# An attention and expert kernel: the first transposed score of a unit goes ahead of the burst of the product with V on TensorE

## The chip, the cores and the metric

The kernel runs on one core of a Trainium2 chip. Its time is the device time of one execution in microseconds (us), the median of three runs. TensorE (PE) does matrix products and transpositions into the eight PSUM banks, VectorE (DVE) reductions and elementwise work, ScalarE (ACT) exponentials and copies, GpSimd (POOL) smaller elementwise work and gathers, and SyncE (SP) issues DMAs. Each engine executes its own program in the written order and waits on semaphores that others raise.

## The reference

```python
def _L0_attn_ref(content, Wq, Wk, Wv):          # content: 4 x 1024 x 256, 16 heads of 16
    Q = (content @ Wq).reshape(b, n, HEADS, HEAD_DIM)
    K = (content @ Wk).reshape(b, n, HEADS, HEAD_DIM)
    V = (content @ Wv).reshape(b, n, HEADS, HEAD_DIM)
    scores = jnp.einsum('bqhd,bkhd->bhqk', Q, K) / math.sqrt(HEAD_DIM)
    alpha = jax.nn.softmax(scores, axis=-1)      # over all keys
    alpha = jnp.where(causal, alpha, 0)          # the mask comes after the softmax
    return jnp.einsum('bhqk,bkhd->bqhd', alpha, V).reshape(b, n, d)
...
x = x + _layernorm(_L0_attn_ref(_layernorm(x), Wq, Wk, Wv))
x = x + _layernorm(_L0_ffn_ref(_layernorm(x), router_w, w_fc, w_proj))
```

`_L0_ffn_ref` is a layer of 8 experts, of which each token uses its best 2 (256 to 1024, exact gelu, back to 256). Since the mask comes after the softmax, maxima and sums run over all 1024 keys, also those above the diagonal.

## The kernel before

**Parts of the program.** A prologue normalizes x and makes Q, K and V in eight chunks; the attention starts within it. The attention runs until about 950 us, with its last groups mixed with the router's work. Then 71 tiles of 128 tokens go through the experts, and the results are added and written.

**Groups and units.** The 64 pairs of batch and head are taken in 16 groups of four heads (`GH`). A pass p of the loop (`groups`, `body`) has 32 units k (`U`). In a unit the engines work on two or three groups at once: plain scores and maxima of group p, transposed scores and the product with V of group p-1 or p-2. `live` says whether a group exists for that. `due(at, k)` gives the numbers of a table that fall into unit k and how many passes back their group is. So the tables `at_chunk`, `at_piece`, `at_m`, `at_poc` and `at_turn` set which unit does what, and the text of `body` on each engine sets the order within a unit.

**What a unit does on PE** (`body` in `block.tensor`):
- at two units of 32 a *turn* (L1313): the finished product with V is transposed;
- at twelve of 32 a *burst* (`pieces`, L1168): one block of 128 keys of four heads times V, in fp32, four heads side by side in 32 columns of the array each, into bank 7. The bursts are numbered 0 to 11 and stand in units 13, 16, 18, 21, 24, 26, 29, and 0, 2, 5, 8, 10 of the next pass. It waits for the exponentials (`s_expB`), for masked copies of POOL (`s_mask`), and at numbers 0 and 8, which start a new half, for DVE's copy of bank 7 (`s_poc`, made at L1760);
- the first *transposed score* (`chunk(p, u, *todo[0])`, L1140), here called A: keys x queries, 512 columns, bf16;
- the pair of *plain scores* of one head and 128 queries (L1326), here S, into banks 0 and 1 or 2 and 3 by turns. It waits for the maximum of two units before (`s_max`). DVE takes the row maximum of the pair (L1786);
- at units 1, 9, 17 and 25 the *transposition of the maxima* of one head (L1337), whose three bf16 parts POOL has made (L762 to L768). ACT copies it out (L962), POOL spreads it (L775) into extra rows of Q, by which a transposed score comes out with its maximum subtracted;
- the second transposed score, here B (L1140, or L1133, a corner of which only the sum is wanted).

ACT takes the exponential of every transposed score: L979 into SBUF for the product, L974 in place for the corners, with the sum by an accumulator read. In its own program of a unit the copy of the maxima (L962) stands ahead of the exponentials of A and B.

**The ring of banks.** A, B, the turns and the transposed maxima share banks 4, 5 and 6. `ring_entries` lists them in the order turn, A, maxima, B for each unit, and `ring_banks` gives each the bank that was used longest ago. Before a matmul into such a bank `ring_free` waits for whoever reads the earlier entry: `s_expB` (exponential), `s_mtc` (copy of the maxima) or `s_norm` (the turn's reader). As a rule the bank is that of the third entry before. A turn keeps its bank for four more entries. The list holds no bursts, which have bank 7.

In a unit without maxima the entries are A, B; so the third entry before an A is the B of two units before. Behind a unit with maxima, whose entries are A, maxima, B, it is the A of that unit. Bursts 2, 5, 8 and 11 are in units 18, 26, 2 and 10, each directly behind one with maxima.

Of the kernel before, what the change touches and what calls it, by code (L numbers as in the profile page):

```python
# [5 lines left out]
def sandwich(nc, x_d, wq_d, wk_d, wv_d, router_d, wfc_d, wproj_d, out_d):  # L6
# [41 lines left out]
    with ctx:  # L48
# [169 lines left out]
        def bk(i):  # L218
            return ps[:, i, :]
# [138 lines left out]
        def diagonal(b):  # L358

            i, hf = BURSTS[b]  # L360
            return hf == i // 4
# [10 lines left out]
        def chunk_of(b, hl):  # L372

            n = GH * b + hl
            return 4 * (n // 3) + n % 3

        def is_corner(c):

            return c % 4 == 3
# [9 lines left out]
        def segments(b, piece):  # L389

            up = upper(b)
            out = [("n", 0, up)] if up else []
            if up < 512:
                out.append(("v", up, 512))
            if diagonal(b):
                out.append(("d", up - P, up))
            return out
# [6 lines left out]
        def due(at, k):  # L404

            return [(n, x // U) for n, x in enumerate(at) if x % U == k]
# [3 lines left out]
        def live(p, back):  # L410

            return not isinstance(p, int) or 0 <= p - back < NGR
# [66 lines left out]
        def wait_pos(eng, s, v):  # L479

            if isinstance(v, int) and v <= 0:
                return
            eng.wait_ge(s, v)
# [58 lines left out]
        def ring_bank(kind, g, x):  # L542

            return RING_BANK[kind, g, x]
# [533 lines left out]
        def _(pe):  # L1078
# [36 lines left out]
            def ring_free(kind, g, x):  # L1115
                if RING_USER[kind, g, x] is None:
                    return
                last, g, x = RING_USER[kind, g, x]
                if last == "chunk":
                    pe.wait_ge(s_expB, NCH * g + x + 1)  # L1120
                elif last == "turn":
                    pe.wait_ge(s_norm, 2 * g + x + 1)
                else:
                    pe.wait_ge(s_mtc, GH * g + x + 1)

            def chunk(p, u, c, back):
                if not live(p, back):
                    return
                g, v = p - back, (u - back) % NSL
                ring_free("chunk", g, c)  # L1130
                if is_corner(c):
                    hl, i = divmod(c // 4, HQ)
                    nc.tensor.matmul(bk(ring_bank("chunk", g, c)), qs[v][0:MROW + MR, hl, i * P:(i + 1) * P],  # L1133
                                     ks[v][0:MROW + MR, hl, 512:1024], start=True, stop=True).then_inc(s_ST, 1)
                    return
                b, hl = divmod(3 * (c // 4) + c % 4, GH)
                i, hf = BURSTS[b]
                if b == 0:
                    pe.wait_ge(s_ex, GH * g + hl + 1)
                nc.tensor.matmul(bk(ring_bank("chunk", g, c)), ks[v][0:MROW + MR, hl, i * P:(i + 1) * P],  # L1140
                                 qs[v][0:MROW + MR, hl, hf * 512:(hf + 1) * 512],
                                 start=True, stop=True).then_inc(s_ST, 1)

            def pieces(p, u, k):
                for n, back in due(at_piece, k):
                    if not live(p, back):
                        continue
                    b, piece = divmod(n, NPC)
                    g, v, (i, hf) = p - back, (u - back) % NSL, BURSTS[b]
                    et, out = et_sb[b % NET], bk(7)  # L1150
                    if isinstance(g, int) and g == 0 and n == 0:
                        pe.wait_ge(s_poz, 1)
                    if b == 0 and piece == 0:
                        pe.wait_ge(s_vc, g + 1)
                    if i == 0 and piece == 0:
                        j = HALVES.index(hf)
                        wait_pos(pe, s_poc, 2 * g + j)
                    if piece == 0:
                        pe.wait_ge(s_expB, NCH * g + (chunk_of(b, GH - 1) + 1))
                    for n, (kind, q0, q1) in enumerate(segments(b, piece)):  # L1160
                        if kind == "d":
                            pe.wait_ge(s_mask, NDG * g + sum(diagonal(x) for x in range(b + 1)))
                        for hl in range(GH):
                            rows, lhs, rhs = {
                                "v": (VW, vh[v][:, hl, i, :], et[:, hl, q0:q1]),
                                "n": (VW, vone[:, :], et[:, hl, q0:q1]),
                                "d": (DH, vh[v][:, hl, i, 0:DH], md_sb[b % NET][:, hl, :])}[kind]
                            ins = nc.tensor.matmul(out[32 * hl:32 * hl + rows, q0:q1], lhs, rhs,  # L1168
                                                   start=(i == 0 and piece == 0 and n == 0), stop=False, skip_group_check=True)
                    if piece == NPC - 1:  # L1170
                        ins.then_inc(s_pv, 1)
# [117 lines left out]
            def body(p, u, units=range(U)):  # L1289
                for k in units:  # L1290
                    if at_tail(AT_LIST, p, k):
                        list_early()
                    for g in tail(at_count, p, k):
                        count(g)
                    if at_tail(AT_TURN0, p, k):
                        transpose_x(0, 0)
                    for hf in range(2):
                        if at_tail(AT_FIRST[hf], p, k):
                            first_half(0, 0, hf)
                    for n in tail(at_turn_x, p, k):  # L1300
                        turn_x(*divmod(n, KC))
                    for i in tail(at_logits, p, k):
                        logits(i)
                    for i in tail(at_back, p, k):
                        turn_back(i)
                    for j, back in due(at_turn, k):
                        if not live(p, back):
                            continue
                        hf = HALVES[j]
                        pe.wait_ge(s_poc, 2 * (p - back) + (j + 1))  # L1310
                        ring_free("turn", p - back, j)
                        for t in range(HQ):
                            ins = nc.tensor.transpose(bk(ring_bank("turn", p - back, j))[:, t * P:(t + 1) * P],  # L1313
                                                      po_sb[:, (HQ * hf + t) * P:(HQ * hf + t + 1) * P], ident[:, :])
                        ins.then_inc(s_T4, 1)
                    pieces(p, u, k)
                    todo = due(at_chunk, k)
                    chunk(p, u, *todo[0])
                    if live(p, 0):
                        hl, i = divmod(k, QT)  # L1320
                        if k == 0:
                            pe.wait_ge(s_ld[u], 16 * 2 * TERMS * ((p - u) // NSL + 1) if isinstance(p, int) else
                                       (16 * 2 * TERMS // NSL) * (p + (NSL - u)))
                        wait_pos(pe, s_max, U * p + k - 1)
                        for hf in range(2):
                            ins = nc.tensor.matmul(bk(2 * (k % 2) + hf), qs[u][0:SROWS, hl, i * P:(i + 1) * P],  # L1326
                                                   ks[u][0:SROWS, hl, hf * 512:(hf + 1) * 512], start=True, stop=True)
                        ins.then_inc(s_S, 1)
                    for hl, back in due(at_m, k):
                        if not live(p, back):  # L1330
                            continue
                        h = GH * (p - back) + hl
                        pe.wait_ge(s_sp, 4 * h + 4)
                        turned[0] += 1
                        if p - back:
                            ring_free("maxima", p - back, hl)
                        nc.tensor.matmul(bk(turn_bank(hl, p - back))[MROW:MROW + MR, 0:P],  # L1337
                                         mparts[:, hl % 2].rearrange("p s i -> p (s i)"), identb[:, :],
                                         start=True, stop=True).then_inc(s_mtp, 1)
                    for c, back in todo[1:]:  # L1340
                        chunk(p, u, c, back)
# [630 lines left out]
```

## Time and profile before

| | |
|---|---|
| median of three runs | 1500.67 us (1499.77 to 1502.28) |
| profiled execution | 1502.44 us, its span 1500.5 us |
| mean granted TensorE clock | 0.979 |
| busy: PE, DVE, ACT, POOL | 93%, 60%, 54%, 42% of the span |
| attention's steady part, 400 to 600 us, busy of 200 us | PE 192.87, DVE 177.80, ACT 162.57, POOL 99.58 |
| one group of heads, 391.76 to 440.04 us | 48.28 us |
| expert part, 1040 to 1100 us | PE busy 60.00 of 60 us |

A row of the timeline gives start, length, engine, line, operation, output <- input, and how many instructions are merged in it. A bracket tells how long the engine had idled before it and what ended that. PE's ends are modelled: a matmul of 512 columns shows 0.38 us, though the next one starts 0.22 us behind it. So on PE distances are read from start to start.

### The profile page before, as it was taken

To read this page: it belongs to the slowest core of one execution; us is meant where nothing else is said; L and a number is where in the kernel's file an instruction comes from. 1 tells how busy PE (TensorE), PEld (TensorE's weight loads), DVE (VectorE), ACT (ScalarE), POOL (GpSimd) and SP (SyncE) were. 2 spreads that over 40 slices of the span, in tenths; PEclk is the share of its full clock that TensorE was granted. 3 is DMA by queue.
4 is the path that set the end of the run, shared out by engine and by line. 5 is a ranking of instruction groups with operands and counts; after the bars stand their busy time and mean duration, and the time that the engine had idled before them with its cause. 6 is when DMAs were issued, how large, how long until landed. Compare 5 with 4: busy or idle time off the path is not lost.

```text
span 1500.5 us, 28701 instructions
## 1 busy us (share of the span) xinstructions
PE 1388.9 (93%) x9774; PEld 828.8 (55%) x9775; DVE 903.0 (60%) x1710; ACT 807.1 (54%) x1757; POOL 625.9 (42%) x749
## 2 busy tenths in 40 slices
PE   6788899999999999999999987999999999999990
PEld 3444233333333333333333333999999999999980
DVE  4587788888988898889988977751111111111115
ACT  4454777777887878888888885311111111111114
POOL 3244444544454545544454523333333333333325
PEclk9999999999999999999999998999999999999995
DMA  3766732023320333122322243666666666666647
GB/s 119 163 156 137 253 43 43 12 33 43 43 35 9 43 43 44 17 27 43 43 35 65 63 136 121 173 171 180 182 189 180 176 179 178 188 188 175 178 113 227
DMA packets 100405, 166.85 MB, mean 111 GB/s; under 512 B 12400, under 2 KB 67568, under 8 KB 100304
## 3 DMA queue, kind: packets, MB, share of 16 engines
q1 hardware_dynamic: 86192, 146.08, 36.6%
q0 software_dynamic: 13632, 18.69, 7.7%
q10 hardware_dynamic: 480, 0.79, 0.3%
q8 instruction: 56, 0.92, 0.3%
q14 instruction: 45, 0.37, 0.1%
HBM read 130.76 MB, written 34.77 MB: 110 GB/s over the span
## 4 chain that ended last, share of the span: by engine, by line
PE 73%; DVE 16%; issue 4%; POOL 2%; ACT 2%; DMA 2%; ACTq 0%; POOLq 0%; DVEq 0%
PE ps L1268 17%; PE ps L1284 16%; PE ps L1168 12%; PE ps L1326 11%; DVE negmax L1786 9%; PE ps L1140 9%; PE ps L1133 2%; PE ps L1101 2%; DVE wfc L1760 1%; POOL wfc L871 1%; PE ps L1257 1%; ACT yx L886 1%; PE ps L1110 1%; DMA arena<-qk_parts 1%; POOL x L736 1%
## 5 line engine op out<-in xcount | busy, mean ns | idle before, releaser
L1786 DVE TENSOR_REDUCE negmax<-ps 128x1 f32<-128x1024 f32 x512 | 605.9, 1218 | 115.7 <-PE ps L1326 115.3
L979 ACT ACTIVATE wfc<-ps 128x512 f32<-128x512 f32 x768 | 430.6, 597 | 137.0 <-PE ps L1140 130.7
L1034 ACT ACTIVATE wfc<-ps 128x512 f32<-128x512 f32 x142 | 84.8, 597 | 422.8 <-PE ps L1268 399.8
L1268 PEld LDWEIGHTS ps<-yx,wfc 128*128 128x128 f32 x2272 | 265.5, 193 | 3.9 <-issue 0.6
L1268 PE MATMUL ps<-yx,wfc 128*128 128x128 f32 x2272 | 266.8, 276 | 0.0
L796 POOL TENSOR_TENSOR wfc<-wfc,causal 128x512 f32<-128x512 f32 x128 | 162.7, 1271 | 227.3 <-issue 97.9
L1284 PE MATMUL ps<-arena,wfc 128*128 x1136 | 257.2, 379 | 0.1
L859 POOL DMA_INDIRECT expert_out<-wfc,rt x71 | 112.9, 1590 | 300.8 <-DVE wfc L1722 289.1
L1326 PE MATMUL ps<-arena 96*128 96x512 bf16 x704 | 211.9, 382 | 16.4 <-DVE negmax L1786 8.5
L1284 PEld LDWEIGHTS ps<-arena,wfc 128*128 128x128 f32 x1136 | 210.3, 190 | 26.3 <-issue 0.6
L1140 PE MATMUL ps<-arena 120*128 120x512 bf16 x528 | 193.4, 387 | 3.0 <-ACT wfc L979 2.0
L1168 PE MATMUL ps<-wfc 128*16 128x128 f32 (+4 forms) x2304 | 161.2, 382 | 0.1
L1722 DVE TENSOR_SCALAR wfc<-ps,rt 128x256 f32<-128x256 f32 x71 | 34.3, 484 | 203.1 <-PE ps L1284 203.1
L974 ACT ACTIVATE ps<-ps 128x512 f32<-128x512 f32 x256 | 152.1, 594 | 7.0 <-PE ps L1133 0.7
L1710 DVE SCALAR_TENSOR_TENSOR rt<-yx,rt 128x1 f32 (+1 forms) x71 | 15.5, 219 | 200.0 <-PE ps L1257 200.0
L1140 PEld LDWEIGHTS ps<-arena 120*128 120x128 bf16 x528 | 50.7, 97 | 124.9 <-ACT wfc L979 47.6
L1326 PEld LDWEIGHTS ps<-arena 96*128 96x128 bf16 x704 | 62.9, 98 | 95.2 <-DVE negmax L1786 33.5
L1168 PEld LDWEIGHTS ps<-wfc 128*17 128x17 f32 (+1 forms) x2304 | 59.7, 97 | 81.6 <-issue 42.0
L1168 PE MATMUL ps<-wfc,vone 128*17 128x128 f32 (+3 forms) x1024 | 95.4, 445 | 8.8 <-DVE wfc L1760 8.8
L1326 PE MATMUL ps<-wfc 96*128 96x512 bf16 x320 | 95.8, 380 | 3.7 <-DVE negmax L1786 3.5
L1140 PE MATMUL ps<-wfc 120*128 120x512 bf16 x240 | 88.0, 383 | 0.7 <-ACT wfc L979 0.3
L775 POOL TENSOR_TENSOR arena<-mT,dmask 24x1024 bf16<-24x1024 bf16 x44 | 83.4, 1895 | 12.1 <-ACT mT L962 9.8
(212 smaller groups left out, 1271.0 us busy)
## 6 DMA issues: line engine op xcount, KB each, us to landing
wfc<-in_L_ffn_w_fc SPq DMA_DIRECT2D x71, 1024.0 KB
arena<-qk_parts SPq DMA_DIRECT2D x126, 128.0 KB, 5.3
qk_parts<-x SPq DMA_DIRECT2D x32, 384.0 KB, 2.8
arena<-in_L_ffn_w_proj SPq DMA_DIRECT2D x8, 1024.0 KB, 8.2
wfc<-qk_parts SPq DMA_DIRECT2D x60, 128.0 KB, 5.5
expert_out<-rt SPq DMA_DIRECT2D x3, 1408.0 KB, 12.1
yx<-in_L_attn_content SPq DMA_DIRECT2D x8, 512.0 KB, 4.4
x<-in_L_attn_content SPq DMA_DIRECT2D x1, 4096.0 KB, 14.1
```

The lines of the kernel that those rows point to most:

```text
L775: pool.tensor_tensor(qs[(u - back) % NSL][MROW:MROW + MR, hl, :] .rearrange("p (i q) -> p i q", i=QT), mT[MROW:MROW + MR, :].unsqueeze(1). ...
L796: pool.tensor_tensor(md_sb[b % NET], et_sb[b % NET][:, :, q:q + P], causal[:, :].unsqueeze(1).to_broadcast([P, GH, P]), ALU.mult).then_inc ...
L859: pool.indirect_dma_start(out=ys_d, in_=yslot[t % 2], in_offset=None, out_offset=bass.IndirectOffsetOnAxis(ap=tok[:, t:t + 1], axis=0), co ...
L974: nc.scalar.activation(bank, bank, ACT.Exp, accum_out=den_u[:, (u - back) % NSL, hl, i:i + 1]).then_inc(s_expB, 1)
L979: nc.scalar.activation(et_sb[b % NET][:, hl, :], bank, ACT.Exp).then_inc(s_expB, 1)
L1034: nc.scalar.activation(hidT[s][:, 4 * hf:4 * hf + 4, :], bk(1 + hf).rearrange("p (c t) -> p c t", c=4), ACT.Gelu).then_inc(s_ge, 1)
L1140: nc.tensor.matmul(bk(ring_bank("chunk", g, c)), ks[v][0:MROW + MR, hl, i * P:(i + 1) * P], qs[v][0:MROW + MR, hl, hf * 512:(hf + 1) * 512 ...
L1168: ins = nc.tensor.matmul(out[32 * hl:32 * hl + rows, q0:q1], lhs, rhs, start=(i == 0 and piece == 0 and n == 0), stop=False, skip_group_ch ...
L1268: ins = nc.tensor.matmul(bk(1 + hf)[:, c * P:(c + 1) * P], w1[s][:, kc * FF + (4 * hf + c) * P:kc * FF + (4 * hf + c + 1) * P], xsT[:, kc, :],
L1284: ins = nc.tensor.matmul(bk(5 + s)[:, 0:D], hidT[s][:, c, :], arena[:, ds(off + c * D, D)], start=(c == 0), stop=(c == FC - 1))
L1326: ins = nc.tensor.matmul(bk(2 * (k % 2) + hf), qs[u][0:SROWS, hl, i * P:(i + 1) * P], ks[u][0:SROWS, hl, hf * 512:(hf + 1) * 512], start=T ...
L1786: nc.vector.tensor_reduce(negmax[:, hl % 2, i:i + 1], ps[:, 2 * (k % 2):2 * (k % 2) + 2, :], AX.XY, ALU.max, negate=True).then_inc(s_max, 1)
```

## The change

In PE's `body`, `pieces` goes behind the first `chunk` of the unit. Nothing else is changed; the ring's list, the units of all operations and the programs of the other four engines are the same.

```diff
                         ins.then_inc(s_T4, 1)
-                    pieces(p, u, k)
                     todo = due(at_chunk, k)
                     chunk(p, u, *todo[0])
+                    pieces(p, u, k)
                     if live(p, 0):
```

Only the twelve units with a burst look different. PE at burst 5, which is behind a unit with maxima, before (from A of the unit with maxima; `wfc` and `arena` are the buffers of this group's operands, in brackets the semaphores that a row waits for):

```order
L1140 MATMUL ps<-arena 128x512 [waits s_expB]
L1326 MATMUL ps<-wfc 128x512 [waits s_max]
L1326 MATMUL ps<-wfc 128x512
L1337 MATMUL ps<-identb,mparts 24x128 [waits s_expB,s_sp]
L1140 MATMUL ps<-arena 128x512 [waits s_expB]
L1168 MATMUL ps<-wfc,vone 17x256 [waits s_expB]
L1168 MATMUL ps<-wfc,vone 17x256 x3
L1168 MATMUL ps<-wfc 17x256 x4
L1168 MATMUL ps<-wfc 16x128 [waits s_mask]
L1168 MATMUL ps<-wfc 16x128 x3
L1140 MATMUL ps<-arena 128x512 [waits s_expB]
L1326 MATMUL ps<-wfc 128x512 [waits s_max]
```

The same place now:

```order
L1140 MATMUL ps<-arena 128x512 [waits s_expB]
L1326 MATMUL ps<-wfc 128x512 [waits s_max]
L1326 MATMUL ps<-wfc 128x512
L1337 MATMUL ps<-identb,mparts 24x128 [waits s_expB,s_sp]
L1140 MATMUL ps<-arena 128x512 [waits s_expB] x2
L1168 MATMUL ps<-wfc,vone 17x256 [waits s_expB]
L1168 MATMUL ps<-wfc,vone 17x256 x3
L1168 MATMUL ps<-wfc 17x256 x4
L1168 MATMUL ps<-wfc 16x128 [waits s_mask]
L1168 MATMUL ps<-wfc 16x128 x3
L1326 MATMUL ps<-wfc 128x512 [waits s_max]
```

A of the burst's unit has joined the B ahead of it, and the burst is followed by S. Each of the two scores has a wait of its own; A's is for the exponential of the first row shown.

PE at burst 8, which starts a half and waits for the copy of bank 7, before:

```order
L1337 MATMUL ps<-identb,mparts 24x128 [waits s_expB,s_sp]
L1140 MATMUL ps<-arena 128x512 [waits s_expB]
L1168 MATMUL ps<-wfc,vone 17x128 [waits s_expB,s_poc]
L1168 MATMUL ps<-wfc,vone 17x128 x3
L1168 MATMUL ps<-wfc 17x384 x4
L1168 MATMUL ps<-wfc 16x128 [waits s_mask]
L1168 MATMUL ps<-wfc 16x128 x3
L1140 MATMUL ps<-arena 128x512 [waits s_expB]
L1326 MATMUL ps<-arena 128x512 [waits s_max]
```

And now:

```order
L1337 MATMUL ps<-identb,mparts 24x128 [waits s_expB,s_sp]
L1140 MATMUL ps<-arena 128x512 [waits s_expB] x2
L1168 MATMUL ps<-wfc,vone 17x128 [waits s_expB,s_poc]
L1168 MATMUL ps<-wfc,vone 17x128 x3
L1168 MATMUL ps<-wfc 17x384 x4
L1168 MATMUL ps<-wfc 16x128 [waits s_mask]
L1168 MATMUL ps<-wfc 16x128 x3
L1326 MATMUL ps<-arena 128x512 [waits s_max]
```

Here too A stands ahead of the burst and so ahead of its wait for `s_poc`.

## Rows read from the trace of the kernel before

**Rows 1.** Page: busy us (share of span), instructions of each engine

```profile
PE 1388.9 (93%) x9774; PEld 828.8 (55%) x9775; DVE 903.0 (60%) x1710; ACT 807.1 (54%) x1757; POOL 625.9 (42%) x749
```

**Rows 2.** Windows: stretch, length, busy us (instructions) by engine, clock, DMA

```profile
391.76:440.04 48.28, 46.57 (x349) 16.60 (x348) 42.96 (x56) 39.28 (x89) 24.36 (x34) 1.00 0.25 34
...
875.00:900.00 25.00, 22.35 (x200) 9.32 (x199) 17.35 (x124) 20.84 (x52) 2.56 (x2) 1.00 0.12 31
```

**Rows 3.** Groups by line, 400 to 600: busy us, mean ns | idle, releaser

```profile
L1786 DVE TENSOR_REDUCE negmax<-ps 128x1 f32<-128x1024 f32 x133 | 157.6, 1216 | 20.9 <-PE ps L1326 20.9
L979 ACT ACTIVATE wfc<-ps 128x512 f32<-128x512 f32 x200 | 112.6, 597 | 33.2 <-PE ps L1140 31.5
```

**Rows 4.** Timeline of PE around burst 5: start, length, line, operation

```profile
609.49 0.23 PE L1337 MATMUL ps<-identb,mparts 128*24 128x128 bf16 x1
609.69 0.39 PE L1140 MATMUL ps<-arena 120*128 120x512 bf16 x1
610.01 0.63 PE L1168 MATMUL ps<-wfc,vone 128*17 128x256 f32 x8
...
611.22 0.39 PE L1140 MATMUL ps<-arena 120*128 120x512 bf16 x1
611.45 0.60 PE L1326 MATMUL ps<-arena 96*128 96x512 bf16 x2
...
613.80 0.38 PE L1133 MATMUL ps<-arena 120*128 120x512 bf16 x1
```

**Rows 5.** Timeline of ACT around burst 5

```profile
609.75 0.26 ACT L962 CAST mT<-ps 24x128 bf16<-24x128 f32 x1
610.04 1.09 ACT L979 ACTIVATE wfc<-ps 128x512 f32<-128x512 f32 x2
...
612.79 0.19 ACT L974 ACTIVATION_READ_ACCUMULATOR ps<-ps 128x1 f32 x1
612.88 1.08 ACT L979 ACTIVATE wfc<-ps 128x512 f32<-128x512 f32 x2
```

**Rows 6.** Timeline of PE's weight loads around burst 5

```profile
613.04 0.10 PEld L1140 LDWEIGHTS ps<-arena 120*128 120x128 bf16 x1 [0.41 <-ACT ps L974]
```

**Rows 7.** Timeline of DVE around burst 5

```profile
612.08 2.36 DVE L1786 TENSOR_REDUCE negmax<-ps 128x1 f32<-128x1024 f32 x2 [0.42 <-PE ps L1326]
```

**Rows 8.** Timeline of PE around bursts 2, 8 and 11

```profile
598.03 0.39 PE L1140 MATMUL ps<-arena 120*128 120x512 bf16 x1
...
621.25 0.39 PE L1140 MATMUL ps<-arena 120*128 120x512 bf16 x1
622.16 0.41 PE L1168 MATMUL ps<-wfc,vone 128*17 128x128 f32 x8 [0.53 <-DVE wfc L1760]
...
633.87 0.39 PE L1140 MATMUL ps<-arena 120*128 120x512 bf16 x1
...
635.62 0.60 PE L1326 MATMUL ps<-wfc 96*128 96x512 bf16 x2
```

**Rows 9.** Timeline of ACT around bursts 2 and 8

```profile
598.42 1.09 ACT L979 ACTIVATE wfc<-ps 128x512 f32<-128x512 f32 x2
...
621.59 1.09 ACT L979 ACTIVATE wfc<-ps 128x512 f32<-128x512 f32 x2
```

**Rows 10.** Timeline of DVE around burst 11, an early and a late pass

```profile
300.13 1.23 DVE L1786 TENSOR_REDUCE negmax<-ps 128x1 f32<-128x1024 f32 x1 [0.99 <-PE ps L1326]
...
635.79 0.90 DVE L1570 TENSOR_SCALAR mv<-mv 128x2 f32<-128x2 f32 x1
636.61 1.21 DVE L1786 TENSOR_REDUCE negmax<-ps 128x1 f32<-128x1024 f32 x1
```

**Rows 11.** Line 1337: count, least/median/most ns, first and last start

```profile
L1337 PE MATMUL ps<-identb,mparts x64: 226/226/283, 86.6 to 862.3; 128*24 128x128 bf16 x64
```

**Rows 12.** Timeline of PE, pairs of scores one of which waits

```profile
592.44 0.81 PE L1140 MATMUL ps<-arena 120*128 120x512 bf16 x2
...
612.75 0.68 PE L1140 MATMUL ps<-arena 120*128 120x512 bf16 x2
```

## The prediction, made before the changed kernel ran

> **What bounds the kernel now.** A unit is one of the 32 steps of a group of four heads; A and B are the two transposed scores that a unit issues, S its pair of plain scores, and a burst is the product with V, which twelve of the 32 units have. I read the busy line first: TensorE (PE) is busy 93% of the span, VectorE (DVE) 60%, ScalarE (ACT) 54% [rows 1]. Then one group of heads as a stretch of time: in 48.28 us PE is busy 46.57, DVE 42.96, ACT 39.28 at the full granted clock [rows 2]. So PE leads, but with two engines close behind it, and what matters is which wait each place has. The groups by line show two kinds of idling: DVE waits for S 20.9 us in 200, and ACT's exponentials wait for A or B 31.5 us in the same 200 [rows 3]. Both come from the bursts: PE spends 1.2 us on a burst in which it feeds neither. The timeline of one such place shows it in numbers: B at 609.69, burst at 610.01, A at 611.22, S at 611.45 [rows 4], and DVE takes up that S after 0.42 us of idling [rows 7]. From there DVE runs maxima without a gap, and PE's next scores wait for them. A delay of S behind a burst is therefore a delay of everything.
>
> **What the change moves.** In each burst unit the row was B(before), burst, A, S. It becomes B(before), A, burst, S. No instruction is added or removed, and S still stands behind both. So S comes earlier only if a wait of the burst is filled by A, and later if A itself has to wait, because A's wait was so far hidden under the burst. What A waits for is its PSUM bank. The ring has three banks, and A takes the one of the third entry before it.
>
> *Eight of the twelve bursts (0, 1, 3, 4, 6, 7, 9, 10): nothing.* The third entry before A is as a rule the B two units back. Burst 6 is the latest kind: B starts at 613.80, the two exponentials from 612.88 last 1.08, so the bank is free at 613.96, 0.16 behind B [rows 4, 5]. A wait is over 0.06 us behind its releaser (accumulator read from 612.79 for 0.19, ends 612.98, weight load at 613.04) [rows 5, 6]. So A may start 0.22 behind B, which is the pace of scores anyway (A to S is 0.23, 611.22 to 611.45). The step from a bf16 score to the fp32 burst costs 0.32 (609.69 to 610.01) [rows 4], now behind A and before behind B: the same. Cost 0, bounds 0.01 either way for each, so 1 us in all. The burst itself ends 0.22 later. Those who wait for its end have cover: ACT needs it three bursts on, and DVE's copy of bank 7 comes behind a maximum of the same unit. At burst 11 the end, 0.23 ahead of S at 635.62, moves by 1.01 to 636.4, and that maximum runs from 636.61 for 1.21 [rows 8, 10].
>
> *The four bursts behind a unit that transposes maxima (2, 5, 8, 11).* The maxima take a ring bank too, between A and B. The third entry before A is then the A of the unit just before, and ACT handles the maxima's copy ahead of that A. Burst 5: maxima on PE at 609.49, ACT's copy 609.75, then two exponentials from 610.04 in 1.09; one is 0.60 (597 ns), so the bank is free at 610.64, and A starts at 610.70, 1.01 behind B [rows 3 to 5]. So far the burst hid this (A at 611.22). The burst starts 0.32 later, at 611.02 instead of 610.01; S follows without A's 0.23 (611.22 to 611.45). S is late by 1.01 - 0.23 = **0.78 us**.
> Burst 2: exponentials from 598.42, first ends 599.02, A at 599.08, 1.05 behind B at 598.03: **0.82** [rows 8, 9].
> Burst 8: here the burst itself waits, for DVE's copy of the product's bank, and starts 0.91 behind B (621.25 to 622.16). A could start at 621.59 + 0.60 + 0.06 = 622.25, the burst at 622.57: 0.41 late, less 0.23: **0.18** [rows 8, 9]. The wait that one would like A to fill is too short by 0.09.
> Burst 11: same pattern as burst 5 on PE and ACT, so 0.78. But from the seventh pass of the loop on, DVE has layer-norm work there: a 0.90 us operation from 635.79, and the maximum only at 636.61 [rows 10]. S started at 635.62 and its pair was through 0.60 later, at 636.22; the normal step from there to DVE is 0.03 (611.45 + 0.60 to 612.08) [rows 4, 7, 8]. So 0.36 of the delay is absorbed, **0.42** remains. In the early passes DVE waits 0.99 us for that S, so nothing is absorbed [rows 10].
>
> *How often.* There are 64 transpositions of maxima, the last at 862.3 [rows 11]. Five have no burst in the next unit (they stand in the first 42 units). Of the other 59, burst 2 and burst 5 have 15 each, burst 8 has 15 of which the last comes when no S is left, burst 11 has 14: 4 without and 10 with the layer-norm work.
> Sum: 15 x 0.82 = 12.3; 15 x 0.78 = 11.7; 14 x 0.18 = 2.5; 4 x 0.78 = 3.1; 10 x 0.42 = 4.2. Together **33.8 us later**.
>
> *What could give some back.* ACT gets A 1.2 us earlier in the eight harmless bursts, so later A's wait less for their bank. Such waits show as pairs of scores that last 0.81 or 0.68 instead of 0.60 [rows 12]: one of 0.21 and three of about 0.08 in a group, 0.45 us, 7 us over sixteen groups. But behind the 0.81 pair DVE is still busy with an earlier maximum, and behind the 0.68 pairs S waits for DVE's maximum as well; I count 0, with 7 as the bound. In the tail behind the last S, where the last group's bursts stand, PE is busy 22.35 of 25 us and ACT 20.84 [rows 2]: neither is full, and the chain goes through several engines. A ahead of a waiting burst saves at most its own 0.23 at each of twelve bursts, 3 us; A waiting in front of a burst costs at most what pairs of rows 12 show, 0.21 each, 3 us too. I take -1, bounds -3 and +3.
> All together: 33.8 - 1 - about 1 for rounding an exponential up to 0.60 where the trace's pairs (1.09) put its end a little earlier = **+32 us**. The profiled execution took 1502.44 us (span 1500.5), so its like would be 1534.4; the median of the runs is 1500.67, 1.8 below, and gives **1532.5**.
>
> **A rule weighed.** In [rows 6] the load behind a waiting score comes only when that wait is over, and the step into a burst is 0.32 rather than 0.22 each time. The Trainium skill ("TensorE: Matmul & The Clock Gate", part 3, "The mechanism") says that PE's queue pulls weight loads ahead of matmuls in flight. By that rule the burst's loads would go ahead of a waiting A and the 0.32 would be 0.22 at the 59 places: 6 us less, about 1526. The trace's 0.32 stands even where nothing waits, so I don't use it.
>
> **The rivals.**
> 1. *No absorption* (0.07). DVE's slack at burst 11 vanishes, because its 0.90 us operation starts after an S-bound maximum. Then ten times 0.36 is added, and the tail goes to its upper bound, 4 above my value: 1532.5 + 3.6 + 4 = 1540. Against it: that operation waits for nothing late, and the maximum before it belongs to the S of the unit before.
> 2. *Partly given back* (0.10). ACT's head start shortens the waits of rows 12 after all, 7 us, and the tail saves its 3, 2 more than I took: 1532.5 - 9 = 1523.5. Against it: DVE sets S there.
> 3. *Hidden* (0.03). The wait of A is covered because the bank is free sooner than I say, i.e. ACT takes the exponential of A ahead of the maxima's copy. Then the four terms vanish: 1500. Against it: the copy stands first in ACT's program and in the rows (609.75, then 610.04).
> 4. *Faster* (0.04). ACT's starvation is what counts: fed through the bursts, it frees the banks early everywhere, the pairs of rows 12 run at 0.60, and the burst's own wait (0.53 idle at burst 8 [rows 8]) is filled by A. Worth 7 us for the pairs and 14 x 0.23 = 3 for burst 8: 1490. It decides only if A's bank is free less than 0.17 us behind B (0.23 less 0.06) at bursts 2, 5, 8 and 11; the rows say 0.95 to 0.99.
>
> **How the numbers follow.** My case has 0.76: its own range is 1526 to 1537. With rivals 1 and 2 the range is 1520 to 1540 (3.5 below rival 2, should the waits pass on in part only), which leaves out 0.1. A measurement of this kernel can tell 0.2%, 3 us. Faster 0.04, within 0.2% 0.03, slower 0.93.
>
> **What would show it.** Right: in the profile after, at the four places A starts about 1.0 us behind B with PE idle some 0.6 to 0.8 us for ACT, and the burst 0.32 behind A; S of bursts 2 and 5 reaches DVE about 0.8 us later than before; the stretch of one late group is 48.3 + 0.82 + 0.78 + 0.18 + 0.42 = 50.5 us; at the other eight bursts nothing but the order changes, and the expert part behind the attention is shifted whole. Wrong: a group of 48.3 us or less, A starting 0.22 behind B after a transposition of maxima, or PE's waits for DVE shrinking by as much as its waits for ACT grow.

## The result, and the profile after

| | before | after |
|---|---|---|
| median | 1500.76 us (1499.77 to 1502.28, 4 runs) | 1539.24 us (1535.35 to 1540.00, 4 runs) |
| profiled execution, span | 1502.44, 1500.5 us | 1539.98, 1538.0 us |
| mean granted clock | 0.979 | 0.981 |
| one late group of heads | 48.28 us | 50.53 us |
| last S starts at | 858.84 us | 894.53 us |

The ratio is 1.0246 [1.0234, 1.0258]: slower, as forecast (1532.5, range 1520 to 1540), but by 38.5 us instead of 31.8. (The quotient of the two medians is 1.0256; by the recorded ratio the loss is about 37 us. The 1500.67 given earlier is the median of three of these four runs.) The page of the kernel after, busy time by engine, answers to [rows 1]:

```profile
PE 1401.3 (91%) x9774; PEld 830.1 (54%) x9775; DVE 905.1 (59%) x1710; ACT 791.7 (51%) x1757; POOL 624.1 (41%) x749
```

The instructions are as many as before, in a longer span. One late group, as a stretch of time (columns as in [rows 2]):

```profile
405.07:455.60 50.53, 47.33 (x350) 16.64 (x348) 43.00 (x56) 38.12 (x88) 24.27 (x34) 1.00 0.22 32
```

DVE's 43.00 us of work is what it was, at the same full clock; the group is 2.25 us longer around it. Groups by line, 415 to 615 us:

```profile
L1786 DVE TENSOR_REDUCE negmax<-ps 128x1 f32<-128x1024 f32 x128 | 151.6, 1216 | 29.4 <-PE ps L1326 29.4
L979 ACT ACTIVATE wfc<-ps 128x512 f32<-128x512 f32 x191 | 105.3, 598 | 12.2 <-PE ps L1140 11.6
L974 ACT ACTIVATE ps<-ps 128x512 f32<-128x512 f32 x64 | 37.9, 593 | 34.7 <-PE ps L1133 34.7
L1140 PE MATMUL ps<-arena 120*128 120x512 bf16 x103 | 36.4, 383 | 6.1 <-ACT wfc L979 6.0
```

Compare with [rows 3]. L979 idles 12.2 us instead of 33.2, which alone would look like a success: ACT is fed earlier. But the corner's exponential L974 (1.8 us idle in the same length before) now idles 34.7, so ACT's idling has moved and grown. L1140 (0.2 us idle in the same length before) waits 6.1 us for ACT, and DVE's wait for S has risen from 20.9 to 29.4.

PE around burst 5, against [rows 4]:

```profile
633.14 0.23 PE L1337 MATMUL ps<-identb,mparts 128*24 128x128 bf16 x1
633.34 0.39 PE L1140 MATMUL ps<-arena 120*128 120x512 bf16 x1
634.34 0.39 PE L1140 MATMUL ps<-arena 120*128 120x512 bf16 x1 [0.61 <-ACT wfc L979]
634.65 0.63 PE L1168 MATMUL ps<-wfc,vone 128*17 128x256 f32 x8
...
635.86 0.61 PE L1326 MATMUL ps<-arena 96*128 96x512 bf16 x2
```

ACT there, against [rows 5], and DVE, against [rows 7]:

```profile
633.40 0.26 ACT L962 CAST mT<-ps 24x128 bf16<-24x128 f32 x1
633.68 1.08 ACT L979 ACTIVATE wfc<-ps 128x512 f32<-128x512 f32 x2
```

```profile
636.51 3.48 DVE L1786 TENSOR_REDUCE negmax<-ps 128x1 f32<-128x1024 f32 x3 [1.21 <-PE ps L1326]
```

A starts 1.00 us behind B, at 634.34. That is 0.66 behind the start of the two merged exponentials at 633.68: one exponential of 0.60 and the 0.06 of a wait. The burst stands 0.31 behind A. From B to S it is now 2.52 us; before, 1.76. DVE idles 1.21 us instead of 0.42. The other three places, PE at bursts 2, 8 and 11 against [rows 8]:

```profile
620.87 0.39 PE L1140 MATMUL ps<-arena 120*128 120x512 bf16 x1
621.91 0.39 PE L1140 MATMUL ps<-arena 120*128 120x512 bf16 x1 [0.64 <-ACT wfc L979]
622.23 1.05 PE L1168 MATMUL ps<-wfc 128*17 128x512 f32 x8
...
645.70 0.39 PE L1140 MATMUL ps<-arena 120*128 120x512 bf16 x1
646.69 0.39 PE L1140 MATMUL ps<-arena 120*128 120x512 bf16 x1 [0.61 <-ACT wfc L979]
647.01 0.41 PE L1168 MATMUL ps<-wfc,vone 128*17 128x128 f32 x8
...
658.52 0.39 PE L1140 MATMUL ps<-arena 120*128 120x512 bf16 x1
659.52 0.39 PE L1140 MATMUL ps<-arena 120*128 120x512 bf16 x1 [0.61 <-ACT wfc L979]
659.84 1.05 PE L1168 MATMUL ps<-wfc,vone 128*17 128x512 f32 x8
```

All show A 1.0 us behind B. At burst 8 the burst no longer waits for the copy of bank 7, but it starts 1.31 behind B; before, 0.91. DVE at burst 11, against [rows 10]:

```profile
660.45 0.85 DVE L1570 TENSOR_SCALAR mv<-mv 128x2 f32<-128x2 f32 x1
661.68 1.23 DVE L1786 TENSOR_REDUCE negmax<-ps 128x1 f32<-128x1024 f32 x1 [0.38 <-PE ps L1326]
```

The maximum starts 3.16 behind B (661.68 against 658.52). Before it was 2.74 (636.61 against 633.87). The difference is 0.42, so the layer-norm operation absorbs what was forecast.

A table by quarter of a group keeps the four places apart: the time from S of unit 1 to S of unit 9, 17, 25 and the next 1. Each quarter holds one of the four bursts. The quarters are read as start differences of S in the timeline of PE, in an early pass (the fifth) and a late one (the twelfth).

| quarter (burst) | before, early / late | after | only the four | only the eight |
|---|---|---|---|---|
| 1 to 9 (8) | 12.62 / 12.62 | +0.20 / +0.20 | +0.19 / +0.18 | +0.02 / +0.01 |
| 9 to 17 (11) | 12.05 / 12.38 | +0.78 / +0.49 | +0.78 / +0.45 | 0.00 / -0.03 |
| 17 to 25 (2) | 11.14 / 11.71 | +0.84 / +0.75 | +0.81 / +0.81 | +0.02 / -0.01 |
| 25 to 1 (5) | 11.56 / 11.56 | +0.80 / +0.80 | +0.78 / +0.77 | +0.02 / +0.02 |
| group | 47.37 / 48.27 | +2.62 / +2.25 | +2.56 / +2.21 | +0.06 / -0.01 |

### The profile page after: what moved, and what is told of

Same layout as the page of the kernel before. It is cut to its first block, busy times and chain, and to the rows that moved or that the text cites. A ratio compares the mean times of both kernels' runs of the same rounds, so it can differ in the third digit from the quotient of the medians.

```text
span 1538.0 us, 28701 instructions
## 1 busy us (share of the span) xinstructions
PE 1401.3 (91%) x9774; PEld 830.1 (54%) x9775; DVE 905.1 (59%) x1710; ACT 791.7 (51%) x1757; POOL 624.1 (41%) x749
## 4 chain that ended last, share of the span: by engine, by line
PE 75%; DVE 11%; ACT 5%; issue 4%; POOL 2%; DMA 2%; ACTq 0%; POOLq 0%; DVEq 0%
PE ps L1268 16%; PE ps L1284 15%; PE ps L1326 13%; PE ps L1168 13%; PE ps L1140 9%; DVE negmax L1786 5%; ACT wfc L979 3%; PE ps L1133 3%; PE ps L1101 2%; POOL wfc L871 1%; PE ps L1257 1%; PE ps L1337 1%; PE ps L1110 1%; ACT yx L886 1%; POOL x L736 1%
## 5 line engine op out<-in xcount | busy, mean ns | idle before, releaser
L979 ACT ACTIVATE wfc<-ps 128x512 f32<-128x512 f32 x768 | 423.6, 599 | 64.8 <-PE ps L1140 62.0
L1034 ACT ACTIVATE wfc<-ps 128x512 f32<-128x512 f32 x142 | 84.8, 597 | 422.4 <-PE ps L1268 422.4
L974 ACT ACTIVATE ps<-ps 128x512 f32<-128x512 f32 x256 | 152.2, 594 | 131.7 <-PE ps L1133 131.7
L1140 PE MATMUL ps<-arena 120*128 120x512 bf16 x528 | 184.6, 385 | 26.7 <-ACT wfc L979 26.0
L1326 PEld LDWEIGHTS ps<-arena 96*128 96x128 bf16 x704 | 53.3, 98 | 126.5 <-DVE negmax L1786 56.1
L1140 PEld LDWEIGHTS ps<-arena 120*128 120x128 bf16 x528 | 51.0, 98 | 124.1 <-ACT wfc L979 63.0
L1140 PE MATMUL ps<-wfc 120*128 120x512 bf16 x240 | 84.5, 385 | 14.3 <-ACT wfc L979 13.5
```

Source lines behind the costliest of these rows:

```text
L974: nc.scalar.activation(bank, bank, ACT.Exp, accum_out=den_u[:, (u - back) % NSL, hl, i:i + 1]).then_inc(s_expB, 1)
L979: nc.scalar.activation(et_sb[b % NET][:, hl, :], bank, ACT.Exp).then_inc(s_expB, 1)
L1034: nc.scalar.activation(hidT[s][:, 4 * hf:4 * hf + 4, :], bk(1 + hf).rearrange("p (c t) -> p c t", c=4), ACT.Gelu).then_inc(s_ge, 1)
```

## The experiments

Quarter differences below are taken as in that table. The median of the kernel before on the same chip was 1501.78 us beside the runs of A first at eight, at four, the exponential first, and the tail; 1501.83 beside burst 8 alone, the exponential first in the kernel before, and both kernels with S, burst, A at four and twelve units; 1502.56 beside the last four.

### Which bursts cost

```diff
-                    pieces(p, u, k)
                     todo = due(at_chunk, k)
+                    ahead = k in (13, 16, 21, 24, 29, 0, 5, 8)
+                    if not ahead:
+                        pieces(p, u, k)
                     chunk(p, u, *todo[0])
+                    if ahead:
+                        pieces(p, u, k)
```

> A ahead of the burst only at the eight bursts that do not follow a transposition of maxima (units 13, 16, 21, 24, 29, 0, 5, 8); the other four as before. Theory (the cost is A's wait for the bank that ACT frees late behind the maxima's copy): at these eight A's bank is free 0.2 us behind B or earlier, so no cost: 0 to +3 us, 1501 to 1504, a group of heads 48.3 us. Rival (any A ahead of a burst costs, by the load of weights or by the burst ending later): two thirds of the +38, about 1526.

Measured: 1501.03 us, ratio 1.0000 [0.9991, 1.0009]. The counterpart has `ahead = k in (18, 26, 2, 10)`:

> A ahead of the burst only at the four bursts behind a transposition of maxima (units 18, 26, 2, 10). Theory: nearly all of the change's cost, by its terms 2.2 us in a late group and 2.6 in an early one, 34 us and what the tail adds: 1534 to 1538, a late group 50.5 us. Rival (spread over all bursts): a third, about 1513.

Measured: 1534.60 us, ratio 1.0216 [1.0201, 1.0231]. A late group, as a stretch, of the kernel with the eight:

```profile
391.06:439.32 48.26, 46.75 (x349) 16.66 (x348) 42.89 (x56) 38.36 (x89) 24.29 (x34) 1.00 0.24 34
```

And of the kernel with the four:

```profile
403.97:454.47 50.50, 47.25 (x350) 16.59 (x349) 43.03 (x56) 39.13 (x89) 24.32 (x34) 1.00 0.25 32
```

The four bursts behind a transposition of maxima carry it all. The eight are free, though ACT gets their A 1.2 us sooner. ACT's lower busy time (38.36, after 38.12, before 39.28) is no gain of time: the group of 48.26 us is as long as before. One of the four alone, `ahead = k == 2`, is burst 8, where I had asked whether A fills the burst's own wait:

> A ahead of the burst only at burst 8 (unit 2), the one whose burst waits for DVE's copy of bank 7 anyway. Theory: A's bank is free 0.94 us behind B, later than the burst's own wait ends, so A fills nothing and costs 0.18 us 14 or 15 times: +2.7, 1503.4. Rival (A fills the burst's wait of 0.6 us): 0.23 gained each time, -3.3, 1497.4.

Measured: 1504.01 us, ratio 1.0012 [1.0003, 1.0021]; group +0.18 / +0.15, all of it in the quarter of burst 8. With ACT's order as it is, A does not fit into that wait. The change in the tail alone, `ahead = p >= NGR`, which leaves the sixteen passes with plain scores as they were:

> A ahead of the burst only from the 17th pass on, that is in the tail where no plain scores are left. In the changed kernel's trace the delay grows by 2 us there. Theory (A's waits in front of bursts add up in the tail): +2 us, 1503. Rival (the tail's 2 us come from the other phase against the clock's half-speed stretches and the chains with DMA): 0 or less, 1500 to 1501.

Measured: 1502.32 us, ratio 1.0003 [0.9994, 1.0011]. The interval, -0.9 to +1.7 us, leaves out the 2 us of the theory: the tail costs and gives nothing that can be told apart.

### The wait itself: which of ACT's instructions stands first

The kernel after, with ACT's exponential of A ahead of its copy of the transposed maxima (L962), which before stood ahead of both exponentials of its unit:

```diff
-                    for hl, back in due(at_m, k):
+                    def copy_m():
+                        for hl, back in due(at_m, k):
...
-                    for c, back in due(at_chunk, k):
+                    for n_c, (c, back) in enumerate(due(at_chunk, k)):
+                        if n_c == 1:
+                            copy_m()
```

> The changed kernel, but ACT takes the exponential of A ahead of the copy of the transposed maxima in the units that have one, so that the bank is freed earlier; same work. Theory: the bank is free about 0.55 us behind B instead of 0.95 to 0.99, A starts at about 0.6, so S is late by 0.4 at bursts 2 and 5, nothing or 0.2 earlier at burst 8, 0.4 or nothing at burst 11: about a third of the cost stays, 1512 to 1517. Rival (the wait has another releaser than that exponential, such as the copy itself or POOL): no change, 1539, or more since the copy comes later.

Measured: 1509.71 us, ratio 1.0049 [1.0035, 1.0064]. Timeline of PE at burst 2, with lines 4 higher (L1144 is the score, L1172 the burst, L1330 S):

```profile
651.15 0.23 PE L1341 MATMUL ps<-identb,mparts 128*24 128x128 bf16 x1
651.31 0.85 PE L1144 MATMUL ps<-arena 120*128 120x512 bf16 x2
652.09 1.05 PE L1172 MATMUL ps<-wfc 128*17 128x512 f32 x8
653.07 0.61 PE L1330 MATMUL ps<-wfc 96*128 96x512 bf16 x2
```

Timeline of ACT there (L983 the exponential, L963 the copy):

```profile
651.12 0.59 ACT L983 ACTIVATE wfc<-ps 128x512 f32<-128x512 f32 x1
651.74 0.26 ACT L963 CAST mT<-ps 24x128 bf16<-24x128 f32 x1
```

In the kernel before, ACT also idled ahead of the copy, until PE had transposed the maxima:

```profile
598.14 0.26 ACT L962 CAST mT<-ps 24x128 bf16<-24x128 f32 x1 [0.21 <-PE ps L1337]
```

The exponential now ends at 651.71. B and A are one row now; its length puts A at 651.31 + 0.85 - 0.38 = 651.78, which is 0.47 behind B instead of 1.04. The quarters cost +0.26 / +0.21 (burst 2), +0.29 / +0.29 (burst 5), +0.26 / -0.01 (burst 11), -0.20 / -0.20 (burst 8); in the kernel after they cost +0.84 / +0.75, +0.80 / +0.80, +0.78 / +0.49 and +0.20 / +0.20. PE's order is that of the kernel after, and the last S is 6.6 us late instead of 35.7: the other 29 come from the order of ACT's program. That is more than the copy itself. The exponential of A starts 0.19 ahead of B (651.12 against 651.31) instead of 0.39 behind it (598.42 against 598.03, 621.26 against 620.87). Of these 0.58 us, 0.28 are the copy, and 0.21 (0.15 in the kernel after) are ACT's idle time ahead of it. What stays is A's 0.47 less the 0.23 that it no longer takes behind the burst. The 1509.71 lies below the 1512 to 1517 that were expected, since S is late by 0.2 to 0.3 and not by 0.4. The same edit in the kernel before:

> The kernel before with ACT's exponential of A ahead of the copy of the transposed maxima. Theory: there the burst hides A's wait, and B behind the maxima waits for another bank, so nothing is gained: 0, within 3 us of 1500.7. Rival (the bank's late release holds PE before too): up to -10.

Measured: 1501.99 us, ratio 0.9998 [0.9990, 1.0007], group 0.00 / -0.02. So it gains nothing by itself; it only frees the bank that a sooner A wants.

### Is a sooner S worth anything?

If a delay of S is a delay of everything, an S ahead of the burst should gain. At the four units the order B, S, burst, A, in the kernel before:

```diff
-                    pieces(p, u, k)
                     todo = due(at_chunk, k)
-                    chunk(p, u, *todo[0])
+                    late = live(p, 0) and k in (18, 26, 2, 10)
+                    if not late:
+                        pieces(p, u, k)
+                        chunk(p, u, *todo[0])
                     if live(p, 0):
...
+                    if late:
+                        pieces(p, u, k)
+                        chunk(p, u, *todo[0])
```

> The kernel before, but at the four bursts behind a transposition of maxima (2, 5, 8, 11) the order is B, S, burst, A: the plain scores, whose maximum of two units before is done 0.26 us behind B there, go ahead of the burst and A stays behind it. Theory: DVE is fed over the burst (it idled 0.42 to 0.99 us at each), PE waits 0.1 less in the units behind bursts 2, 5 and 11, and at burst 8 S fills 0.44 of the 0.6 us wait: 0.65 to 0.75 a group, -10 us, about 1490. Rival (PE has no slack but the pairs, and ACT starves longer since A comes 0.44 later): 0 or slower, 1500 to 1506.

Measured: 1501.73 us, ratio 0.9998 [0.9990, 1.0007]; quarters in the late pass -0.23 (burst 8), 0.00 (11), -0.31 (2), +0.35 (5), and in the early one -0.22, +0.02, +0.26, +0.34. The gain did not come. But the equal time hides two differences: an early group is 0.41 us longer than before and a late one 0.20 shorter, and over five early and ten late groups they cancel. Why the quarter of burst 2 gains late and loses early was not traced. Timeline of PE around burst 5 (L1328 is S):

```profile
657.28 0.59 PE L1328 MATMUL ps<-wfc 96*128 96x512 bf16 x2
...
658.33 0.61 PE L1328 MATMUL ps<-wfc 96*128 96x512 bf16 x2
658.87 0.63 PE L1168 MATMUL ps<-wfc,vone 128*17 128x256 f32 x8
...
660.07 0.39 PE L1140 MATMUL ps<-arena 120*128 120x512 bf16 x1
...
660.73 0.60 PE L1328 MATMUL ps<-wfc 96*128 96x512 bf16 x2
...
661.75 0.39 PE L1140 MATMUL ps<-arena 120*128 120x512 bf16 x1 [0.21 <-ACT ps L974]
661.98 0.60 PE L1328 MATMUL ps<-wfc 96*128 96x512 bf16 x2
```

S comes 1.05 behind the S before it; in the kernel before it is 2.48 (657.24 to 659.72). But the following S stands behind the burst all the same, at 3.45 (before 3.35), and the one after it at 4.70 (before 4.40), because A went to ACT late and a later score waits 0.21 for it. (In the version below, with A ahead of the burst, the same S is 4.41 behind again, 649.06 to 653.47.) At burst 5 the burst has only moved from ahead of one S to ahead of the next. With this order at all twelve bursts:

> The same at all twelve bursts: B, S, burst, A. At the eight others the maximum for which S waits is done only 0.6 to 1.0 us behind B, so S itself would wait ahead of the burst. Theory: 8 x 0.6 us of waiting in a group against 3 us of waits for DVE that go: +1 to +3 us a group, 1515 to 1545. Rival (with S always first DVE never starves, and the group shrinks towards DVE's 43 us): -2 a group, 1470.

Measured: 1536.85 us, ratio 1.0235 [1.0220, 1.0250], group +2.83 / +2.36. The number is in the expected range, but not by the mechanism that was expected. Between 400 and 600 us, PE's matmuls idle 8.6 us for ACT in 32 waits and only 2.0 for DVE; in the kernel before it is 4.4 for DVE and 2.1 for the copy of bank 7. So what shows is scores that wait for ACT, and hardly S that waits ahead of the burst. These waits make some 1 us of the 2.4 in a late group; the rest was not assigned. One of them, on PE in unit 1:

```profile
644.99 0.39 PE L1140 MATMUL ps<-arena 120*128 120x512 bf16 x1 [0.27 <-ACT ps L974]
```

### A version that beats both

S ahead of the burst, A too, but behind S so that its bank has come free (B, S, A, burst at the four units), with ACT's exponential first:

```diff
...
+                    if late:
+                        chunk(p, u, *todo[0])
+                        pieces(p, u, k)
```

> Two edits to the kernel before: ACT takes the exponential of A ahead of the copy of the maxima (so that the bank is free about 0.5 us behind B instead of 0.95), and at the four bursts behind a transposition of maxima PE's order is B, S, A, burst. Theory: S is ready 0.26 behind B and covers what is left of A's wait, so nothing waits in front of the burst, both DVE and ACT are fed over it, and burst 8's 0.6 us wait for the copy of bank 7 is filled: 0.5 to 0.9 us a group gained, 1487 to 1493. Rival (as with B, S, burst, A, which moved nothing: PE's later waits for ACT take the gain back): within 3 us of 1501.8.

Measured: 1487.89 us (1487.07 to 1489.79), ratio 0.9901 [0.9886, 0.9916]. A late group as a stretch:

```profile
389.17:436.44 47.27, 46.61 (x349) 16.31 (x348) 42.97 (x56) 38.68 (x89) 24.28 (x34) 1.00 0.23 34
```

Timeline of PE at burst 8 (L1332 S, L1144 score, L1137 corner):

```profile
614.13 0.39 PE L1144 MATMUL ps<-arena 120*128 120x512 bf16 x1
614.45 0.60 PE L1332 MATMUL ps<-wfc 96*128 96x512 bf16 x2
614.89 0.38 PE L1144 MATMUL ps<-arena 120*128 120x512 bf16 x1
615.21 0.41 PE L1172 MATMUL ps<-wfc,vone 128*17 128x128 f32 x8
...
616.41 0.39 PE L1137 MATMUL ps<-arena 120*128 120x512 bf16 x1
```

S and A stand where the burst used to wait for the copy of bank 7. No row here waits, and the corner of the next unit starts 2.28 behind B; before it was 2.78 (621.25 to 624.03). The quarters: -0.50 (burst 8), -0.01 (11, early pass -0.27), -0.56 (2, early -0.03), +0.06 (5). Half of a late group's gain is burst 8's; at burst 5 there is none, and why burst 2 gains late and burst 11 early was not traced. The same order with ACT's program as it was has no run, so what the exponential put first adds to it is not shown. Burst 8 alone in this manner:

> The same two edits, but the order B, S, A, burst at burst 8 alone. Theory (only burst 8 has a wait on PE to fill, 0.6 us): 15 times 0.22 to 0.55, 1493.5 to 1498.5. Rival: nothing.

Measured: 1494.17 us, ratio 0.9945 [0.9931, 0.9958], group -0.50 / -0.50. And burst 8 alone with B, S, burst, A, ACT as in the kernel before:

> The kernel before with B, S, burst, A at burst 8 alone, ACT unchanged. In the trace of the same order at four bursts each group gained 0.23 us at burst 8 and lost or regained as much at the other three. Theory: 15 times 0.23, 3.4 us faster, 1498.4. Rival (given back later in the group): 0.

Measured: 1498.72 us, ratio 0.9970 [0.9958, 0.9982], group -0.22 / -0.22. Timeline of PE there:

```profile
619.99 0.39 PE L1140 MATMUL ps<-arena 120*128 120x512 bf16 x1
620.31 0.61 PE L1328 MATMUL ps<-wfc 96*128 96x512 bf16 x2
620.90 0.41 PE L1168 MATMUL ps<-wfc,vone 128*17 128x128 f32 x8
...
622.34 0.38 PE L1133 MATMUL ps<-arena 120*128 120x512 bf16 x1
622.55 0.60 PE L1313 MATMUL ps<-ident,wfc 128*128 128x128 f32 x4
623.19 0.39 PE L1140 MATMUL ps<-arena 120*128 120x512 bf16 x1
```

The burst is 0.91 behind B, exactly as in the kernel before, and S is inside that time. The corner is 2.35 behind B, 0.43 sooner, but from the turn to the next score it takes 0.64 us instead of 0.44 (624.25 to 624.69 before), so half is left. That A went out late is the likely reason; it was not tried apart.

### The kernel after once more

The same kernel without any edit, on another occasion.

> The changed kernel once more. What is open: its attention is 35.6 us later at the last S, but its end 37.4, though neither the tail's order alone nor the eight harmless bursts cost anything. If the tail's 2 us belong to the order, a second trace shows the last S 35 to 36 later and the end 2 more; if they come from how the tail meets the clock's half-speed stretches and the DMAs, the difference between the two is another one, down to -1.

Measured: 1537.11 us (1536.12 to 1537.39), ratio 1.0229 [1.0215, 1.0243]; its group +2.64 / +2.27, its last S at 894.46 in a span of 1535.4. So attention is as in the first trace, and the part behind it is not: from the last S to the end 641.7 us before, 643.5 in the first trace of after, 641.0 in the second, 640.2 in the kernel with the four.

The two traces of the same program can be laid over each other. They part at one burst 11.5 us behind the last S. Timeline of PE, first trace and second:

```profile
906.06 1.06 PE L1168 MATMUL ps<-wfc,vone 128*17 128x256 f32 x8
...
905.94 0.63 PE L1168 MATMUL ps<-wfc,vone 128*17 128x256 f32 x8
```

The stretch 904 to 910 us as in [rows 2], first trace and second (the clock is the third number from the right):

```profile
904.00:910.00 6.00, 4.93 (x47) 1.83 (x47) 3.45 (x14) 2.94 (x8) 0.95 (x2) 0.72 1.10 357
...
904.00:910.00 6.00, 4.68 (x58) 2.29 (x61) 3.39 (x14) 4.24 (x12) 2.20 (x3) 1.00 1.10 360
```

The granted clock was 0.72 in this stretch of the first trace and 1.00 in the second. From the burst to the next score PE takes 2.27 us instead of 1.21 (906.06 to 908.33, 905.94 to 907.15), and at 910 us the first trace is 1.3 us behind. This is about half of the 2.5 us by which the two tails differ. At 957.21 the first trace has a wait of 1.05 us for DVE that the second does not show. What the other half is made of was not traced further.

## Why the prediction was right, and where its size was off

**The number was close to a miss.** The 1539.24 lies 0.8 us inside the stated range, and above the 1526 to 1537 that the prediction gave for its own case; the second occasion's 1537.11 lies at that edge. The range reached so far only because a rival's 1540 had been included, and that rival's mechanism is not what happened. Direction and mechanism are another matter, since rows and runs show them.

**The mechanism held at every step.** A's distance behind B was worked out as 1.05, 1.01, 1.00 and 1.01 for bursts 2, 5, 8 and 11; it is 1.04, 1.00, 0.99 and 1.00. "The burst 0.32 behind A" is 0.31 to 0.32. The group of 50.5 us is 50.53. That the wait is for ACT, and for ACT's order, is shown by the exponential put first, which takes away 29 of the 35.7 us. The prediction named ACT's copy as what stands ahead of A's exponential; that ACT also idles for PE's transposition ahead of the copy, as at burst 2, it did not say. That only four of twelve bursts matter is shown by the pair of kernels with the four and the eight.

**The terms.** Burst 2: 0.82 forecast, 0.81 in the kernel with the four. Burst 5: 0.78, 0.77. Burst 8: 0.18, 0.18. Burst 11: 0.78 early, 0.78; 0.42 late, 0.45. The absorption by DVE's operation was forecast as 0.36 and is 0.33 there and 0.29 in the kernel after.

**The size was off by three terms of the sum.** The forecast had 32 us; the second execution of after, by its span, has 34.9 and the first 37.5. First, "about 1 for rounding an exponential up to 0.60": this was subtracted without a need, since the terms came out as they stood before it. Second, the small ones, read as the delay of S against the kernel before. From unit 17 of pass 1 on, where the counting begins, the kernel with the four gains 33.9 us of delay up to the last S, for 33.8 forecast. The kernel after gains 34.6 in its first trace and 34.8 in the second. The 0.6 to 0.9 between them go with the eight harmless bursts, forecast "Cost 0, bounds 0.01 either way": 2.62 - 2.56 = 0.06 in an early group, 2.25 - 2.21 = 0.04 in a late one. Ahead of that unit, where no cost was counted, the kernel after is 1.1 and 0.8 us late, and the kernel with the four 0.2. Four parts, 1 us for the rounding, 0.9 for the eight, 0.8 for the start and 0.1 for the four, make the 2.8 us by which the second trace's last S (35.6 late) exceeds 33.8 - 1. Third, the tail, "I take -1, bounds -3 and +3": it was +1.8 in the first trace, -0.7 in the second and -1.5 in the kernel with the four, and the change in the tail alone moves nothing. So -1 lies within the scatter of single traces and no run confirms it; the first profile's +1.8 is its execution's own, with the granted clock's 0.72 in one stretch as about half of the difference to the second.

**The rivals.** The first, *no absorption*, gave 1540, and the median of 1539.24 lies next to it. Its mechanism is false all the same: DVE's maximum is late by 0.42 at burst 11, not 0.78, and the tail's upper bound is not what the change does. The hit of that number is luck. The second, *partly given back*, fails: the eight bursts that feed ACT sooner change a late group by -0.01 us and an early one by +0.06. The third, *hidden*, needs ACT's exponential ahead of its copy; with it the loss is 0.5% and not none. The fourth, *faster*, had a true half: the wait of burst 8 can be filled. S fills it with ACT's order as it is (0.22 us a group), and S and A with the exponential first (0.50). A alone fills it too once the exponential is first, as the -0.20 of that quarter shows. There B and A stand in one row of 0.88 us from 626.50, so A starts at 627.00, 0.50 behind B, and the burst at 627.41, 0.91 behind B as in the kernel before. The prediction's condition, a bank free less than 0.17 us behind B at all four places, was therefore too strict for burst 8: its burst waits until 0.91 anyway, and with 0.32 for the step A may start up to 0.59 behind B.

**The rule weighed.** A burst behind an A that has waited 0.61 us still starts 0.31 behind it (634.34 to 634.65). Timeline of PE's weight loads, the burst's in the kernel after and, at burst 5, that of S in the kernel before:

```profile
634.65 0.13 PEld L1168 LDWEIGHTS ps<-wfc,vone 128*17 128x17 f32 x8 [0.23 <-issue]
...
611.23 0.32 PEld L1326 LDWEIGHTS ps<-arena 96*128 96x128 bf16 x2
```

The burst's load starts with the burst, not ahead of it; the load of S starts 0.22 ahead of S (611.45), beside A (611.22). The Trainium skill ("TensorE: Matmul & The Clock Gate", part 3, "The mechanism") says that PE's queue pulls weight loads ahead of matmuls in flight when the load goes to rows of the array that do not conflict, or to the background weight buffer. The prediction left this condition out. The traces agree with the pull from score to score and show none from a bf16 score to an fp32 burst behind a semaphore wait; why not, no run shows. The 6 us that it would have given back did not appear.

**The missed expectation.** The expectation that S sooner at four units would gain 10 us took S for the only thing that DVE waits for. At burst 5 S is one of a row: to put it ahead of the burst makes the next ones late (3.45 and 4.70 for 3.35 and 4.40). With A ahead of the burst as well the loss goes (4.41), but there is no gain there either; a gain is sure only where something that stood idle is filled, at burst 8.

## What to carry to other kernels

Before an instruction is put ahead of a long one on an in-order engine, find what released its resource and when: a wait hidden under the long instruction becomes everyone's wait. Look for the place's exceptions (here four of twelve, where another operation had shifted the ring of banks by one and the consumer handled a small copy, and waited for it, first), since the common case may well be free. Here the wait was filled by what was already free to go, and the order of the consumer mattered as much as that of the producer: with the exponential ahead of the copy the loss fell from 2.3 or 2.5% to 0.5%. S, then A, then the burst, again with the exponential first, gained 1%; how much of that needs the exponential first is open. And an equal time can be two differences that cancel, so it pays to look at an early and a late group apart.

## What the runs showed of the hardware that was not expected

The part behind the attention took 640.2 to 643.5 us in four traces, though its instructions were the same in number and, in the stretch of the experts, PE was busy throughout. A difference of 2 us in one profile of this kernel is therefore no sign of a cause in its order: the kernel after had medians of 1539.24 and 1537.11 us on two occasions, with intervals of the ratio that overlap. About half of the 2.5 us between its two traces arose where the granted clock was 0.72 in one and 1.00 in the other, in 6 us of the same program. Within the attention the traces repeat far better: quarters of a group agree to 0.02 us between the two traces of the same kernel, which is why the verdicts above lean on them.
